# Dense sampling: y rows by DMA to 24 partitions, their clamp on ScalarE, the x clip on GpSimd, the end of a band in place in PSUM

## What is computed

```python
offsets = conv2d(x, offset_w, offset_b)              # 18 channels: y and x of 9 taps
mod = sigmoid(conv2d(x, mod_w, mod_b))               # 9 channels
sy = base_y + off[:, 0];  sx = base_x + off[:, 1]    # one position per tap and pixel
y0, x0 = floor(sy), floor(sx);  wy1, wx1 = sy - y0, sx - x0
sampled = (1 - wy1) * ((1 - wx1) * g00 + wx1 * g01) + wy1 * ((1 - wx1) * g10 + wx1 * g11)
out = einsum('bckp,ock->bop', sampled, weight) * mod.mean(axis=1) + bias
```

## Time and profile before

| | us |
|---|---|
| median of 3 runs | 3055.5 (3055.1 to 3060.2) |
| the profiled execution | 3057.7 |
| its span, first to last instruction | 3055.6 |
| dense stage of the second group, from the first clear to the end | 2501.3 to 3055.6 |
| TensorE busy | 2441.4 (80%) |
| VectorE, ScalarE, GpSimd busy | 1772.6, 1530.8, 1028.2 |

### The profile page before, as it was taken

One profiled execution on the slowest core, in us unless ns is written; L12 is line 12 of the kernel. 1 busy time (PEld: TensorE's weight loads), 2 busy tenths in 40 slices (PEclk: granted clock), 3 DMA queues, 4 the chain that ended last, 5 costly groups with the idle time before them and its releaser, 6 DMA issues. The chain is left out here.

```text
span 3055.6 us, 98677 instructions
## 1 busy us (share of the span) xinstructions
PE 2441.4 (80%) x44813; PEld 1586.9 (52%) x44813; DVE 1772.6 (58%) x2823; ACT 1530.8 (50%) x1757; POOL 1028.2 (34%) x740
## 2 busy tenths in 40 slices
PE   1774992839999748699999927599995669999998
PEld 0673441527777524355555515477773334555555
DVE  5894656235555464467677661455555535666765
ACT  1222544225555544466666642355555435766665
POOL 0331000035555200555555300455551015555552
PEclk7897996869999969699999958799997787999999
DMA  1577712011111212122221130111113121111221
GB/s 40 161 204 135 107 28 110 3 39 30 28 29 32 73 70 61 48 67 66 69 66 64 52 119 16 36 27 30 27 27 132 25 56 53 66 67 66 68 68 40
DMA packets 221258, 191.40 MB, mean 63 GB/s; under 512 B 77036, under 2 KB 171808, under 8 KB 220832
## 3 DMA queue, kind: packets, MB, share of 16 engines
q1 hardware_dynamic: 220832, 185.02, 22.2%
HBM read 119.96 MB, written 65.01 MB: 61 GB/s over the span
## 5 line engine op out<-in xcount | busy, mean ns | idle before, releaser
L2180 PE MATMUL dense_spread<-dense_cp,kept_spread_yx 32*128 32x512 f32 x2432 | 478.3, 665 | 76.0 <-DVE dense_cp L2339 62.8
L1461 ACT ACTIVATE snake_samp<-snake_s 128x1024 f32<-128x1024 f32 x320 | 321.1, 1023 | 300.7 <-PE snake_s L1391 300.6
L2359 DVE TENSOR_TENSOR dense_hat<-dense_spread,dense_hat 128x1024 f32<-128x1024 f32 x256 | 301.6, 1220 | 236.2 <-PE dense_spread L2180 236.2
L1524 DVE TENSOR_SCALAR snake_hat<-snake_spread 128x1024 f32<-128x1024 f32 x256 | 301.6, 1220 | 206.4 <-PE snake_spread L1369 206.4
L2284 ACT ACTIVATE dense_hat<-dense_spread 128x1024 f32<-128x1024 f32 x256 | 248.5, 1021 | 322.8 <-PE dense_spread L2180 318.5
L1391 PE MATMUL snake_s<-snake_hat,snake_xt 64*64 64x128 f32 x10240 | 338.7, 275 | 19.1 <-ACT snake_samp L1461 18.9
L2230 PEld LDWEIGHTS dense_s<-dense_hat,dense_xt 64*64 64x64 f32 x11264 | 267.9, 134 | 145.5 <-ACT dense_samp L2304 94.6
L2304 ACT ACTIVATE dense_samp<-dense_s 128x864 f32<-128x864 f32 (+1 forms) x384 | 299.3, 834 | 67.0 <-PE dense_s L2230 66.9
L1391 PEld LDWEIGHTS snake_s<-snake_hat,snake_xt 64*64 64x64 f32 x10240 | 286.6, 134 | 85.2 <-issue 42.1
L2230 PE MATMUL dense_s<-dense_hat,dense_xt 64*64 64x108 f32 x11264 | 308.8, 257 | 0.5
L2242 PE MATMUL dense_s<-dense_samp,kept_w_dcn 64*64 64x264 f32 x4608 | 284.9, 388 | 3.6 <-ACT dense_samp L2304 3.6
(11 more groups left out here) (325 smaller groups left out, 3573.0 us busy)
## 6 DMA issues: line engine op xcount, KB each, us to landing
dense_cp<-offs SPq DMA_DIRECT2D x576, 56.0 KB
x<-blur_x SPq DMA_DIRECT2D x16, 1024.0 KB, 5.0
pre<-snake_ob SPq DMA_DIRECT2D x32, 512.0 KB, 4.2
out<-dense_xr SPq DMA_DIRECT2D x64, 256.0 KB, 3.1
gateconv_low<-x SPq DMA_DIRECT2D x24, 512.0 KB, 9.5
dense_cp<-offs SPq DMA_DIRECT2D x256, 48.0 KB
offs<-dcnoff_cm SPq DMA_DIRECT2D x64, 144.0 KB
residual0Silu_x<-x SPq DMA_DIRECT2D x16, 512.0 KB, 8.9
```

What stands on the lines that cost most here:

```text
L1461: act.activation(samp[u % 2][:, :, i * MS:(i + 1) * MS, :, :].rearrange("p b m t h -> p b (m t h)"), sample_at(u, i)[:, :, :], ACT.Copy).t ...
L1524: ins = dve.tensor_scalar(strided(hat[u % 2][:, 0:1], GUARD + (4 * tau + 2 * half) * SW * SR, [[8, 2], [SW * SR, 2], [SR, SW], [1, 8]]), s ...
L2180: return pe.matmul(bank[:, :], k.spread_yx[r, kind, :], cp[u % 2][r, tile, :], start=True, stop=True)
L2359: dve.tensor_tensor(h, p_hat[pair][:, :, :].rearrange("p t (r x) -> p (t r) x", x=W), h, ALU.mult).then_inc(main_ready, 1)
```

## The change

- y no longer goes through TensorE. `load_y` copies each image's y channels, for taps 0 to 3 and 4 to 8 (`PARTS`), to 24 partitions of `ys`, one buffer per part. ScalarE applies Relu with a bias per partition, from `ys` to `hat` (`keep_y`); the upper clamp is a `min` with 1 inside VectorE's product, now a fused instruction. Partitions of a block that are not loaded stay zero.
- x lies as two tiles of adjacent taps in each block, loaded by one copy; `spread_x(u, i)` uses the two blocks 2i and 2i+1, two matmuls on each. `spread_last` is x of the ninth tap and the modulation.
- The clip of x, three tiles at once, is one GpSimd instruction between `stage` and `keep_even`; VectorE has no clip.
- `finish` multiplies in PSUM in place and adds into `mod`, which is stored; `xr` is single. The modulation copy for a band waits for the store of the band two before. Sampling round 1 waits for the whole of `finish`.
- `weigh` is one stretch with 256 columns for 264; `samp` and `mod` have 128 columns for 132.
- `offs` in DRAM is laid out as (16 rows, image, 4 rows, channel, row, column), so that the channels of a band lie together. The store of the offsets keeps its copies and runs of 512 B.
- Tables: `spread_x`, `clip` and `y_shift` for `spread_yx`, `clip` and `row_last`; `w_dcn` keeps 64 columns for 128, through one more diagonal tile and two more small copies. The gather path, not run, rebuilds the wide weights.

```diff
...
+            divide(rest[:, :], 8, 3, number[:, :], low[0][:, :])
+            link(dve.tensor_scalar(k.y_shift[:, :], number[:, :], -1.0, 1.0, ALU.mult, ALU.add))
+            divide(rest[:, :], 4, 7, number[:, :], low[0][:, :])
+            link(dve.tensor_scalar(used[:, :], rest[:, :], 28.0, None, ALU.is_lt))
+            link(dve.tensor_tensor(number[:, :], number[:, :], used[:, :], ALU.mult))
+            link(dve.tensor_tensor(k.clip[:, 0:1], number[:, :], is_last[:, :], ALU.add))
+            link(dve.tensor_tensor(k.clip[:, 1:2], k.clip[:, 0:1], used[:, :], ALU.add))
...
-                    sp.dma_start(offs[0:MOD, :, u * RU + q:(u + 1) * RU:4, :], cm[u % 2][32 * q:32 * q + MOD, :, :, :]).then_inc(stored[u % 2], 16)
+                    sp.dma_start(offs[u, :, :, 0:MOD, q, :].rearrange("b i c w -> c b i w"), cm[u % 2][32 * q:32 * q + MOD, :, :, :]).then_inc(stored[u % 2], 16)
...
+    PARTS = (range(0, 4), range(4, K2))
+    X_LOADS = 6 * 16
+    Y_LOADS = GI * 16
...
-            def load(u):
-                def put(tile, block_, ch, times):
-                    at = offs[ch, 0, 4 * u, 0:1]
-                    sp.dma_start(cp[u % 2][32 * block_:32 * block_ + GI * times, tile, :],
-                                 bass.AP(tensor=at.tensor, offset=at.offset, ap=[[H * W, GI], [0, times], [1, 4 * W]])).then_inc(loaded[u % 2], 16)
-
+            def load_x(u):
                 for i in range(4):
-                    y = offs[2 * i, 0, 4 * u, 0:1]
-                    sp.dma_start(cp[u % 2][32 * i:32 * i + 24, 2, :],
-                                 bass.AP(tensor=y.tensor, offset=y.offset, ap=[[H * W, 2 * GI], [0, 3], [1, 4 * W]])
+                    at = offs[u // 4, 0, u % 4, K2 + 2 * i, 0, 0:1]
+                    sp.dma_start(cp[u % 2][32 * i:32 * i + 28, 0:2, :],
+                                 bass.AP(tensor=at.tensor, offset=at.offset, ap=[[0, 7], [4 * OFF_CH * BX, GI], [1, 2 * BX]])
                                  ).then_inc(loaded[u % 2], 16)
-                for tile in range(2):
-                    for i in range(4):
-                        put(tile, i, K2 + 2 * i + tile, 7)
-                put(3, 0, 2 * K2 - 1, 7)
-                put(3, 1, K2 - 1, 3)
-                sp.dma_start(cp[u % 2][64:64 + GI, 3, :], offs[MOD, :, 4 * u:4 * u + 4, :].rearrange("b h w -> b (h w)")).then_inc(loaded[u % 2], 16)
-
-            sp.wait_ge(ones_set, 1)
-            load(0)
-            load(1)
+                at = offs[u // 4, 0, u % 4, 2 * K2 - 1, 0, 0:1]
+                sp.dma_start(cp[u % 2][0:28, 2, :], bass.AP(tensor=at.tensor, offset=at.offset, ap=[[0, 7], [4 * OFF_CH * BX, GI], [1, BX]])
+                             ).then_inc(loaded[u % 2], 16)
+                sp.dma_start(cp[u % 2][64:64 + GI, 2, :], offs[u // 4, :, u % 4, MOD, :, :].rearrange("b h w -> b (h w)")).then_inc(loaded[u % 2], 16)
+
+            def load_y(u, part):
+                for b in range(GI):
+                    at = offs[u // 4, b, u % 4, PARTS[part][0], 0, 0:1]
+                    sp.dma_start(ys[part][32 * b + 8:32 * b + 32, :, :].rearrange("p t x -> p (t x)"),
+                                 bass.AP(tensor=at.tensor, offset=at.offset, ap=[[0, 24], [1, len(PARTS[part]) * BX]])
+                                 ).then_inc(y_in[part], 16)
+
+            def store(u):
+                sp.wait_ge(out_done, u + 1)
+                sp.dma_start(out_v[:, 4 * u:4 * u + 4, :], mod[u % 2][:, :, :]).then_inc(stored[u % 2], 16)
+
+            sp.wait_ge(cleared, 1)
+            load_x(0)
+            load_y(0, 0)
+            load_y(0, 1)
+            load_x(1)
+            for part in range(2):
+                sp.wait_ge(y_kept[part], 1)
+                load_y(1, part)
+            sp.wait_ge(mod_spread, 1)
+            load_x(2)
             for u in range(NB4):
                 if u + 2 < NB4:
-                    sp.wait_ge(mod_spread, u + 1)
-                    load(u + 2)
+                    for part in range(2):
+                        sp.wait_ge(y_kept[part], u + 2)
+                        load_y(u + 2, part)
                 if u >= 1:
-                    sp.wait_ge(out_done, u)
-                    sp.dma_start(out_v[:, 4 * u - 4:4 * u, :], xr[(u - 1) % 2][:, :, :]).then_inc(stored[(u - 1) % 2], 16)
-            sp.wait_ge(out_done, NB4)
-            sp.dma_start(out_v[:, H - 4:H, :], xr[(NB4 - 1) % 2][:, :, :]).then_inc(stored[(NB4 - 1) % 2], 16)
+                    store(u - 1)
+                if u + 3 < NB4:
+                    sp.wait_ge(mod_spread, u + 2)
+                    load_x(u + 3)
+            store(NB4 - 1)
...
+                pool.memset(ys[i][:, :, :], 0.0)
...
-                if u >= 2:
-                    pool.wait_ge(stored[u % 2], u // 2 * 16)
+                if u >= 1:
+                    pool.wait_ge(out_done, u)
                 r0 = PAD + 4 * u
-                pool.tensor_scalar(xr[u % 2][:, :, :], xn[:, r0:r0 + 4, PAD:PAD + W], k.std[:, :], k.shift[:, :], ALU.mult, ALU.add
+                pool.tensor_scalar(xr[:, :, :], xn[:, r0:r0 + 4, PAD:PAD + W], k.std[:, :], k.shift[:, :], ALU.mult, ALU.add
                                    ).then_inc(x3_ready, 1)
 
+            def clip(u):
+
+                pool.wait_ge(loaded[u % 2], X_LOADS * (u // 2 + 1))
+                x = cp[u % 2][:, :, :].rearrange("p t n -> p (t n)")
+                pool.tensor_scalar(x, x, k.clip[:, 0:1], k.clip[:, 1:2], ALU.max, ALU.min).then_inc(x_clipped, 1)
+
+            pool.wait_ge(cleared, 2)
             stage(0)
+            clip(0)
             for u in range(NB4):
                 if u + 1 < NB4:
                     stage(u + 1)
+                    clip(u + 1)
                 keep_even(u)
-                restore(u)
+                if u >= 1:
+                    restore(u - 1)
+            restore(NB4 - 1)
...
-                return pe.matmul(bank[:, :], k.spread_yx[r, kind, :], cp[u % 2][r, tile, :], start=True, stop=True)
-
-            def spread_y(u, i):
+                return pe.matmul(bank[:, :], k.spread_x[r, kind, :], cp[u % 2][r, tile, :], start=True, stop=True)
+
+            def spread_x(u, i):
 
                 for pair in range(2):
-                    if i == 0:
-                        if pair == 0:
-                            pe.wait_ge(y_clipped, u + 1)
+                    if i == 1:
+                        pe.wait_ge(main_ready, 4 * u + pair + 1)
+                    elif pair == 0:
+                        pe.wait_ge(x_clipped, u + 1)
                         if u > 0:
-                            pe.wait_ge((hat_ready, mod_kept)[pair], u)
-                    else:
-                        pe.wait_ge(main_ready, 4 * u + pair + 1)
+                            pe.wait_ge(hat_ready, u)
+                            pe.wait_ge(mod_kept, u)
+                    elif u > 0:
+                        pe.wait_ge(main_ready, 4 * u)
                     for at in range(2):
-                        ins = spread(p_hat[pair][:, at, :], u, 2 * pair + at, 2, 1 + i)
-                    ins.then_inc(y_spread, 1)
-
-            def spread_x(u, i):
-
-                if i == 0:
-                    pe.wait_ge(x_clipped, u + 1)
-                for pair in range(2):
-                    pe.wait_ge(y_kept, 4 * u + 2 * i + pair + 1)
-                    for at in range(2):
-                        ins = spread(p_hat[pair][:, at, :], u, 2 * pair + at, i, 0)
+                        ins = spread(p_hat[pair][:, at, :], u, 2 * i + pair, at, 0)
                     ins.then_inc(x_spread, 1)
 
             def spread_last(u):
 
                 pe.wait_ge(main_ready, 4 * u + 3)
-                spread(p_hat[0][:, 1, :], u, 1, 3, 1)
-                spread(p_hat[0][:, 0, :], u, 0, 3, 0).then_inc(last_spread, 1)
-                pe.wait_ge(main_ready, 4 * u + 4)
-                spread(p_hat[1][:, 0, :], u, 2, 3, 3).then_inc(mod_spread, 1)
+                spread(p_hat[0][:, 0, :], u, 0, 2, 0).then_inc(last_spread, 1)
+                spread(p_hat[0][:, 1, :], u, 2, 2, 1).then_inc(mod_spread, 1)
...
-                        pe.wait_ge(scale_done, u)
+                        pe.wait_ge(out_done, u)
...
             spread_x(0, 0)
-            spread_y(0, 1)
             spread_x(0, 1)
             spread_last(0)
             for u in range(NB4):
                 more = u + 1 < NB4
                 if more:
-                    spread_y(u + 1, 0)
-                if u > 0:
-                    weigh(u - 1, range(0, 3))
-                if more:
                     spread_x(u + 1, 0)
                 if u > 0:
-                    weigh(u - 1, range(3, K2))
-                if more:
-                    spread_y(u + 1, 1)
+                    weigh(u - 1)
                 sample(u, 0)
-                sample(u, 1)
                 if more:
                     spread_x(u + 1, 1)
+                sample(u, 1)
                 sample(u, 2)
                 sample(u, 3)
                 if more:
```

(49 more changed lines are left out.)

139 lines of the change are left out of this document (53 added, 86 removed).

## The result

The changed kernel takes 3176.52 us, median of 5 runs (3159.79 to 3179.34), against 3055.59 before (5 runs): a ratio of 1.038, 95% interval 1.036 to 1.040. I had forecast 2945 and gave slower 8%. The profiled execution took 3159.8, its span is 3156.5, 100.9 us more than before.

What follows compares the result with a forecast made beforehand. TensorE's issue was taken to bound the dense stages, 15.80 us a band. Bands of 14.5 save 81 us and the two stage starts 29, together 110: 2945 us, range 2898 to 3008 (main case 2920 to 2982).

Steps and rivals of the forecast that it cites:

- TensorE's sum: Dense-stage band on TensorE: stretches of spreading, weighing and sampling sum to 13.39 us, plus 0.45 wait for a copy: 13.85.
- rival (a): TensorE's x spreads: the two blocks do not overlap, 2.9 us a stretch, band 15.8, only the start won: 3026 us; 9%.
- ScalarE and VectorE: Dense-band work: Relu 2.1 and 2.5 us, ScalarE near 11; fused product 1.25, two finishing operations of about 0.75 each.
- GpSimd's clip: Clip of x, 1536 wide, one GpSimd instruction: taken as 2.3 us, between 1.5 and 2.4; GpSimd 10.5 a band.
- the ring: Modulation copy, sampling copies, y parts on ScalarE, then the store's landing, which a later modulation copy awaits: 8.2 us plus D.
- The pace of the y rows: DMA of y rows: 46 us of one engine per MB; part 1 takes 3.75 us on twelve engines.
- D: From the end of ScalarE's y part 1 to the store's landing: 6.3 us taken, floor 5.6; band 14.5.
- Each has some 9 us, so the rows themselves cost nothing: Loads of y parts 0 and 1: each has some 9 us between issue and need, so no cost.
- my top of 9.3: Upper bound of D, the store also waiting for all of part 1's 0.98 MB: 9.3 us, a band of 17.5.
- The start of a stage: From the clear to ScalarE's first sampling copy in each dense stage: 34 us for 49, 14.5 saved per stage.
- The tables and weights: Tables lose some nine short linked operations, weights gain two copies: 1 us either way.
- (c): Rival, slower through the ring: D past 7.6 us puts the band over 15.8; 3063 us, 3131 at the top; 9%.

Runs made afterwards that it cites:

- part 1 small: Against the changed kernel, part 1 of the y rows loads one tap of its five, with the same four issues: 2929.9 us, ratio 0.959.
- the kernel with all three edits: Against the changed kernel: store ahead of part 1 of the y loads, x clip on VectorE behind the last product, sum stored from `xr`: 3019.8 us, ratio 0.989.

## Why the prediction was wrong

Point by point, in its own order.

- **TensorE's sum: right.** 13.85 us forecast; 13.84 with the store first and with part 1 small. Stretches of four x matmuls 1.92 (1.93), weighing and round 0 4.79 (4.80), rounds 1 to 3 with their wait 2.88 (2.81), last spread 1.06 (1.1), last rounds 1.27. The two blocks of 32 partitions do work side by side, as I argued from the earlier trace rows, and rival (a) is dead. That rival's rule in the Trainium skill ("TensorE: Matmul & The Clock Gate", "What overlaps and what doesn't") would give 2.9 a stretch; 1.92 speaks against its strict form.
- **ScalarE and VectorE: right.** Relu 2.0 and 2.43 (2.1, 2.5), fused product 1.217 (1.25), finishing 0.70 and 0.70 (0.75 each).
- **GpSimd's clip: wrong by 3.2 us,** 5.51 for 2.3. I priced max and min by a multiply and add. With part 1 small it cost nothing, with GpSimd at 13.78 of 13.84 us; where GpSimd also waited for stores (the sum in `xr`), the band was 14.8. In the changed kernel the ring hides it.
- **The pace of the y rows, a term of D.** I took 46 us of one engine per MB from the earlier trace rows, where narrow copies of 2 KB pieces run at 24 bytes a nanosecond. The y rows ran at 13. Part 1 has 8 rows on each of 12 engines: 8 x 0.773 = 6.2 us, where I had 3.75. "Each has some 9 us, so the rows themselves cost nothing" held for the wait on the rows themselves (ScalarE waits for y 75.4 us, all in the first two bands of each stage), and not for what stands behind them in the queue.
- **D, and in it the store's landing: the step that failed.** I put D at 6.3 us, "near the floor, since issue and data overlap". It measured 10.1, median of all bands, and 11.1 in the long one shown, beyond my top of 9.3. The four issues were cheaper than I took them, 1.5 us for 2.6; the landing was not 2.6, measured with nothing ahead of it, but 6.9 in the median and 9.5 right behind part 1. That the bytes ahead of the store do it is shown: with the store ahead of them, or most of them left out, D is 5.8 or 5.7 and the loss is gone. Of the 3.8 us that I was short, the slower pace would be 2.5 by my own formula (6.2 for 3.75, an estimate from the packets); the rest is open.
- **A second ring that I had not drawn.** The modulation copy also holds up TensorE's next spread, and with it the weighing, the finish and the next store, with no y part in between. Everything in it but the landing is 8.3 us at full clock (0.61, 1.93, 4.05, 1.41 and the gaps), so a landing over 5.5 us lengthens the band, whatever ScalarE does. The kernels that store from `mod` bear this out: with median landings of 6.4 to 7.1 us their bands are 17.3 to 17.8 on average, with 3.5 to 4.4 they are 13.7 to 14.8. I had named that spread as waiting and did not follow it round.
- **The clock:** the gaps of TensorE cost more than themselves: behind them weighing took 5.2 to 6.5 us, for 4.05. My prices for D had no such term.
- **The start of a stage:** 48.8 us before from clear to first sampling copy, 34 forecast, 43.7 measured (2551.43 to 2595.08). The second band's x landed only at 2582.8, behind the first band's y rows, and its clip took 5.5; the y rows of the second band at 2587.0 and 2592.7.
- **The tables and weights:** I put them at 1 us either way; the part ahead of the first dense stage is 4.0 us shorter.
- **Rivals:** (c) was the right one, with the mechanism, place and sign that I gave, and 3131 as its top against 3176.5. Its 9% rested on "115 us of engine time, under 10 a band even on twelve": a mean load, used against a ring in which what counts is the burst of 0.98 MB right ahead of the store. I had the ring before me and gave it the wrong length.

## What to carry over

A buffer that is turned into the output buffer puts a DMA landing into whatever ring its next writer is in: draw every ring through that writer, the one through an in-order engine's next instruction too. Price a landing with the bytes issued just ahead of it, on whichever queue, and let the small transfer that someone waits for be issued first; here the order of two statements on SP was worth 196 us. Price a DMA by packets that go to a like destination, and an elementwise operation by one with the same operators, not by one of the same form.

## What the hardware showed that I had not expected

- 24 neighbouring partitions of one block of 32, written by 12 DMA engines: 611 ns for 8 KB; every fourth partition: 381. The twelve fit the rule that I cited from the Trainium skill ("DMA: Bandwidth & Descriptors", "Why a DMA increments its semaphore by 16 and not by 1"): in the records 12 such packets are in flight for 70% of the time in which y rows move (400 us of the second stage).
- A store on a queue of its own lands 7.1 us after issue, as late as in the shared one (6.9).
- VectorE's clip of 1536 columns takes 1.08 us beside an idle GpSimd, and up to 2.83 beside GpSimd's difference of two inputs (the kernel with all three edits).
- GpSimd: max and min 3.4 ns a column, multiply and add 0.8 ((1621 - 767) / 1024); VectorE does the max and min over 1536 columns in 1.08 us. The Trainium skill ("GPSIMD Engine Reference", "4.1 Engine selection") calls GpSimd's elementwise operations of one input "roughly line-rate", in one row for add, mul and max. Here max and min take four times what multiply and add take, so it can hold for one of them at most.
- Two-dimensional copies issue on SP in 0.29 to 0.37 us, the three-dimensional ones of x in some 0.75.

The fastest kernel of this study with the reference's output is the changed one with the store issued first: 2980.4 us, 2.4% under the kernel before.
